# Second attention of a small vision tower: the maximum of slot 1 is subtracted by TensorE in PSUM instead of by VectorE, and VectorE copies that slot's transposes

## What is computed

```python
def _L1_attn_ref(x, edge_index, edge_attr, Wq, bq, Wk, bk, Wv, bv, Wo, bo, We, be):
    q = (x @ Wq + bq).reshape(B, N, H, hd)          # B=8 images, N=64 tokens, H=8 heads, hd=8
    k = (x @ Wk + bk).reshape(B, N, H, hd)
    v = (x @ Wv + bv).reshape(B, N, H, hd)
    scores = jnp.einsum('bihd,bjhd->bhij', q, k) / jnp.sqrt(jnp.asarray(hd, x.dtype))
    scores = scores + col_bias[None, :, None, :]     # from edge_attr @ We + be
    attn = jax.nn.softmax(scores, axis=-1)
    out = jnp.einsum('bhij,bjhd->bihd', attn, v).reshape(B, N, D)
    return out @ Wo + bo

h = _L0_tok_ref(...)                       # patch embedding and positions
h = h + _L0_attn_ref(_layernorm(h), ...)   # first attention
h = h + _L0_ffn_ref(_layernorm(h), ...)    # routed feed-forward
h = h + _L1_attn_ref(_layernorm(h), ...)   # second attention: here
h = h + _L1_ffn_ref(_layernorm(h), ...)    # top-2 mixture of 8 experts
```

## Time and profile before

| | |
|---|---|
| median of 3 runs | 74.75 us (74.56 to 74.87) |
| the profiled execution | 74.51 us |
| its span, first to last instruction | 72.7 us |
| outside the span | 1.8 us |
| PE busy | 64.6 us, 89% of the span |
| DVE busy | 41.9 us, 58% |
| ACT busy | 29.2 us, 40% |
| POOL busy | 13.0 us, 18% |
| granted TensorE clock, mean | 0.992 |

### The profile page before, as it was taken

One profiled execution on the slowest core, in us unless ns is written; L12 is line 12 of the kernel. 1 busy time (PEld: TensorE's weight loads), 2 busy tenths in 40 slices (PEclk: granted clock), 3 DMA queues, 4 the chain that ended last, 5 costly groups with the idle time before them and its releaser, 6 DMA issues.

```text
span 72.7 us, 1994 instructions
## 1 busy us (share of the span) xinstructions
PE 64.6 (89%) x843; PEld 39.5 (54%) x843; DVE 41.9 (58%) x108; ACT 29.2 (40%) x63; POOL 13.0 (18%) x29
## 2 busy tenths in 40 slices
PE   3995996999999999989979969799999889999930
PEld 1330554777887585445435645577954285543910
DVE  2590199484799983536642397997540157429430
ACT  0330104404497821296925060488023748530030
POOL 6800094000004920538030000000000030000000
PEclk9999999999999999999999999999999999999996
DMA  0799999900000000000000000000000000000003
GB/s 5 180 394 390 373 224 263 265 16 0 0 9 0 0 9 0 0 0 5 0 0 0 0 0 9 0 9 0 0 9 5 0 0 0 0 0 0 0 0 72
DMA packets 2389, 4.07 MB, mean 56 GB/s; under 512 B 779, under 2 KB 1229, under 8 KB 2381
## 3 DMA queue, kind: packets, MB, share of 16 engines
q1 hardware_dynamic: 1840, 3.55, 16.8%
q10 hardware_dynamic: 509, 0.40, 1.7%
q0 software_dynamic: 32, 0.00, 0.1%
HBM read 3.82 MB, written 0.13 MB: 54 GB/s over the span
## 4 chain that ended last, share of the span: by engine, by line
PE 64%; DVE 13%; DMA 9%; ACT 4%; POOL 3%; issue 3%; DVEq 0%; ACTq 0%; POOLq 0%
PE psum L687 10%; DMA Xt<-in_x_dram 9%; PE psum L681 6%; DVE top L503 3%; POOL WoS L298 3%; PE psum L697 3%; PE psum L893 3%; PE psum L939 3%; PE psum L789 3%; PE psum L740 3%; PE psum L991 3%; PE psum L1032 2%; PE psum L716 2%; DVE E L601 2%; DVE top L599 2%
## 5 line engine op out<-in xcount | busy, mean ns | idle before, releaser
L687 PE MATMUL psum<-warm 128*128 128x512 bf16 x63 | 19.9, 429 | 1.2 <-DVE warm L455 1.2
L687 PEld LDWEIGHTS psum<-warm 128*128 128x128 bf16 x63 | 5.8, 107 | 8.1 <-issue 4.3
L298 POOL TENSOR_TENSOR WoS<-pack_attn,top 128x256 f32<-128x256 f32 x5 | 3.1, 647 | 11.1 <-DVE top L510 11.1
L468 DVE TENSOR_TENSOR onehot<-idb,iota 128x2048 bf16<-128x2048 bf16 x4 | 4.8, 1244 | 0.0
L326 POOL TENSOR_TENSOR resT<-hT,xC 128x256 f32<-128x256 f32 x1 | 0.7, 724 | 20.5 <-DVE xC L630 20.5
L405 ACT ACTIVATE E<-E 128x512 f32<-128x512 f32 x4 | 2.5, 630 | 3.2 <-DVE E L601 3.1
L348 ACT ACTIVATE lv<-psum,eps 128x256 f32<-128x256 f32 x4 | 1.9, 473 | 3.5 <-PE psum L729 0.9
L599 DVE TENSOR_REDUCE top<-psum 128x8 f32<-128x512 f32 x4 | 2.7, 686 | 0.4 <-PE psum L908 0.4
L434 ACT ACTIVATE ge<-psum,pack_moe 128x512 f32<-128x512 f32 x4 | 2.5, 679 | 1.1 <-PE psum L991 1.1
L908 PE MATMUL psum<-kT,qT 9*64 9x64 f32 x128 | 2.1, 231 | 0.9 <-DVE qT L587 0.7
L773 PE MATMUL psum<-top,pack_ident 128*128 128x256 f32 x12 | 2.9, 387 | 0.0
(11 more groups left out here) (200 smaller groups left out, 131.7 us busy)
## 6 DMA issues: line engine op xcount, KB each, us to landing
Xt<-in_x_dram SPq DMA_DIRECT2D x1, 1024.0 KB, 6.4
Xt<-in_x_dram SPq DMA_DIRECT2D x1, 512.0 KB, 7.5
pack_both<-in_both_dram SPq DMA_DIRECT2D x2, 240.2 KB, 8.8
pack_moe<-in_moe_dram SPq DMA_DIRECT2D x1, 450.0 KB, 9.8
pack_mid<-in_mid_dram SPq DMA_DIRECT2D x1, 327.5 KB, 10.0
pack_attn<-in_attn_dram SPq DMA_DIRECT2D x1, 288.0 KB, 8.1
pack_expert<-in_expert_dram SPq DMA_DIRECT2D x2, 130.0 KB, 9.3
pack_wp<-in_wp_dram ACTq DMA_DIRECT2D x1, 192.0 KB, 6.0
```

The source lines that it names most:

```text
L298: gp.tensor_tensor(WoS[:, s, 4 * u:4 * u + 4, :].rearrange("p (b n) d -> p b n d", b=2), bc(WoT[:, 2 * u:2 * u + 2, :], 1, 2), bc(top0[:, ...
L468: ve.tensor_tensor(onehot[:, 16 * k:16 * k + 16, :], bc(idb[:, k, :], 1, 16), iota16[:, :, :], ALU.is_equal).then_inc(s_hot, 1)
L687: mm(B[bank][:, :], lhsT=warm[:, 0:P], rhs=warm[:, :], start=True, stop=True)
```

## The change

Slot 1 alone is treated differently. DVE takes its maximum with the sign turned (`negate`), and does not subtract. A new function `shift1()` on PE, behind `scores1(1)`, multiplies the identity with the negated maximum into banks 0 to 3, columns 128 to 255, accumulating onto the scores. The scores products therefore set their start flag only for the first block of a bank. ACT's `exp1(1)` waits for `shift1()` and reads PSUM. Because PSUM then holds slot 1's scores until that exponential is done, the transposes of slot 0 (bank 2) and `values1` (banks 0 and 1) wait for `exp1(1)`. ACT does `exp1(2)` before `et_copy(0)`; `et_copy(1)` leaves ACT and becomes a DVE copy behind the last subtraction. Two `keep_clock` calls, three dummy products together, are gone.

```diff
@@ ACT @@
             def exp1(s):
-                act.wait_ge(s_sub1, s + 1)
-                sc.activation(E1[:, s, :, :], E1[:, s, :, :], ACT.Exp).then_inc(s_exp1, 1)
+                if s == 1:
+                    act.wait_ge(s_sub1p, 1)
+                    sc.activation(E1[:, 1, :, :].rearrange("p (q g) t -> p q g t", g=2),
+                                  psum[:, 0:4, P:2 * P].rearrange("p q (g t) -> p q g t", t=TOK), ACT.Exp).then_inc(s_exp1, 1)
+                else:
+                    act.wait_ge(s_sub1, max(s, 1))
+                    sc.activation(E1[:, s, :, :], E1[:, s, :, :], ACT.Exp).then_inc(s_exp1, 1)
...
             exp1(0)
             exp1(1)
+            exp1(2)
             et_copy(0)
-            exp1(2)
-            et_copy(1)
             exp1(3)
             et_copy(2)
@@ DVE @@
-                ve.tensor_reduce(top, S, X, ALU.max).then_inc(s_mx1, 1)
+                ve.tensor_reduce(top, S, X, ALU.max, negate=(s == 1)).then_inc(s_mx1, 1)
+                if s == 1:
+                    return
                 dve.wait_ge(s_mx1, s + 1)
                 ve.tensor_tensor(E1[:, s, :, :].rearrange("p (q g) t -> p q g t", g=2), S, bc(top, 3, TOK),
                                  ALU.subtract).then_inc(s_sub1, 1)
...
+            dve.wait_ge(s_et, 2)
+            ve.tensor_copy(ET[:, 1, :, :].rearrange("p q n -> p (q n)"), B[3][:, :]).then_inc(s_et_ev_v, 1)
             dve.wait_ge(s_v1, 2)
@@ PE @@
-                                         rhs=kT1[rows_, g, tok:tok + TOK], start=True, stop=True)
+                                         rhs=kT1[rows_, g, tok:tok + TOK], start=(j == 0 and g == 0), stop=(c == 1),
+                                         skip_group_check=True)
...
+            def shift1():
+
+                pe.wait_ge(s_mx1, 2)
+                for hh in range(4):
+                    ins = mm(B[hh][:, P:2 * P], lhsT=ident, rhs=bc(top1[:, 1, 2 * hh:2 * hh + 2], 2, TOK), start=False, stop=True,
+                             skip_group_check=True)
+                ins.then_inc(s_sub1p, 1)
...
             def values1(c):
-                pe.wait_ge(s_sub1, 2)
+                pe.wait_ge(s_exp1, 2)
...
             def context(c):
...
-                    if s < 3:
-                        pe.wait_ge(s_et_ev_a, s + 1)
+                    if j == 0:
+                        pe.wait_ge(s_et_ev_a, c + 1)
                     else:
-                        pe.wait_ge(s_et_ev_v, 1)
+                        pe.wait_ge(s_et_ev_v, c + 1)
...
             scores1(1)
-            pe.wait_ge(s_sub1, 2)
+            shift1()
+            pe.wait_ge(s_exp1, 2)
             probsT(0)
-            keep_clock(3, 2)
             probsT(1)
             values1(0)
             values1(1)
             pe.wait_ge(s_et_ev_a, 1)
-            keep_clock(2, 1)
             probsT(2)
-            pe.wait_ge(s_sub1, 4)
+            pe.wait_ge(s_sub1, 3)
             pe.wait_ge(s_h2, 1)
             mm(B[6][:, 0:HALF], lhsT=centre[:, :], rhs=hT[2][:, :], start=True, stop=False, skip_group_check=True)
-            pe.wait_ge(s_et_ev_a, 2)
+            pe.wait_ge(s_et_ev_v, 1)
             probsT(3)
```

More of the change, by code:

```diff
@@ L222, in vit_tower @@
         s_v1, s_v1_ev = sem("v1_ps"), sem("v1_ready")
-        s_sc1, s_mx1, s_sub1, s_exp1 = sem("scores1_ps"), sem("max1_done"), sem("shifted1"), sem("exp1_done")
+        s_sc1, s_mx1, s_sub1, s_sub1p, s_exp1 = (sem("scores1_ps"), sem("max1_done"), sem("shifted1"), sem("shifted1_ps"),
+                                                 sem("exp1_done"))
         s_q1_v = sem("q1_ready_dve")
@@ L403, in exp1 @@
             def exp1(s):
-                act.wait_ge(s_sub1, s + 1)
-                sc.activation(E1[:, s, :, :], E1[:, s, :, :], ACT.Exp).then_inc(s_exp1, 1)
+                if s == 1:
[5 more added lines that the diff above has]
+                    sc.activation(E1[:, s, :, :], E1[:, s, :, :], ACT.Exp).then_inc(s_exp1, 1)
             def et_copy(s):
                 act.wait_ge(s_et, s + 1)
-                bank = B[2 + s % 2]
-                sc.activation(ET[:, s, :, :].rearrange("p q n -> p (q n)"), bank[:, :], ACT.Copy).then_inc(s_et_ev_a, 1)
+                sc.activation(ET[:, s, :, :].rearrange("p q n -> p (q n)"), B[2][:, :], ACT.Copy).then_inc(s_et_ev_a, 1)
             exp1(0)
             exp1(1)
+            exp1(2)
             et_copy(0)
-            exp1(2)
-            et_copy(1)
             exp1(3)
```

## The result

The changed kernel takes 77.83 us in the median of four runs (77.47 to 78.84), the kernel before 74.66 beside it (74.56 to 74.87). The ratio is 1.040 (95% interval 1.036 to 1.045), so the change costs 3.0 us, between 2.7 and 3.4. I had said 75.7, at most 76.3: the direction was right, the size wrong by a factor of three.

The account below looks back on a forecast made before the run. It took PE's own work and DVE's softmax, meeting at 50.6, to bound the context stage. Transposes 1.62 later, less 0.66 for dummies, gave +0.96 on 74.75: 75.7, range 75.2 to 76.3.

Parts of the forecast that it names:

- The change's path: On PE ahead of slot 0's transposes: products 1.07, exponential 0.60, wake-up 0.06; 1.62 later, less 0.66 for dummies, +0.96.
- The factor of four: Identity products on PE: by the skill each costs four transposes, 1.76 in all; fell in the dearer-products rival, 8 in 100.
- VectorE gains nothing: DVE's softmax: the removed subtraction's 0.69 becomes idle time, since the third maximum waits for scores1(1); gain taken as 0.
- TensorE's dummies are worth nothing before: Context stage before the change: PE's own work and DVE's softmax, nearly equal in length, meet at 50.6.
- The new waits behind it: Behind slot 0's transposes: DVE's copies and bias additions and ACT's work have 0.5 us or more to spare, adding nothing.
- Clock: Rival: TensorE's clock falls in PE's hole from 48.0 to 48.7; up to 79, or 77 if partly; 5 in 100.
- what the sum puts behind the context: nothing: Behind context(0): nothing hides or adds to the delay, and everything is shifted by the same +0.96.
- rival of a shorter pause: Pause inside scores1(1) gone: DVE's chain 0.5 shorter, 74.25 only if PE's chain also shrinks, otherwise +0.5; 4 in 100.

Follow-up runs that it names:

- e12: Changed kernel with only two of the four identity products and one single-element ScalarE activation more: 75.31 us, ratio 1.008 to the kernel before.
- e14: Changed kernel with twelve tiny TensorE dummies more ahead of the router logits and one single-element ScalarE activation more: ratio 1.012 to the kernel before.
- e4: Kernel before the change, without the three dummies between the transposes: 75.04 us, ratio 1.002.
- e3: Changed kernel with slot 1's subtraction given back to VectorE, all else of the change kept: 75.42 us, ratio 1.006 to the kernel before.
- e8: Kernel before the change, without the six dummies ahead of scores1(1): 76.20 us, ratio 1.017.
- e7: Changed kernel with one dummy fewer ahead of scores1(1) and one single-element ScalarE activation more: profiled execution 76.87 us at a clock of 0.977.
- e9: Changed kernel with one single-element ScalarE activation more behind et_copy(2): profiled execution 77.90 us at a clock of 0.975, another 75.56 at full clock.
- e13: Changed kernel with twelve tiny dummies more ahead of the router logits, where TensorE waits: profiled execution 76.88 us at a clock of 0.977.
- e15: Kernel before the change, with twelve tiny dummies more ahead of the router logits, where TensorE waits: profiled execution 74.99 us.
- e2: Changed kernel without five dummies around the second layer norm, where TensorE waits anyway: profiled execution 76.24 us.
- e6: Changed kernel with one dummy fewer ahead of scores1(1): 77.45 us, ratio 1.034 to the kernel before.

## Why the prediction was right and wrong

**The change's path: right, to 0.03.** Identity products, exponential, wake-up, less three dummies: +0.96 forecast, +0.99 in the trace, and half of the products give 0.45 back (`e12`). That it came as near as 0.03 is in part luck, since small errors cancelled. The products took 1.16 instead of 1.07 (I had built on the 0.63 of four transposes in the earlier trace rows; the four there that stood behind a wait took 0.66), but they started 0.05 earlier behind the scores, and the exponential with its hand-overs took 0.69 instead of 0.70. From the transposes on it was 3.39 (49.33 to 52.72), as forecast. With the side effects out the ratio gives 0.9, within 0.5 to 1.2 (`e14`), which agrees but would not tell 0.96 from 0.6. The factor of four that the Trainium skill gives for the transpose mode ("TensorE: Matmul & The Clock Gate", its section "Terms") would have made the products 1.76 and does not hold: four of them took 1.16, as eight records do, and eight transposes took 1.09.

**VectorE gains nothing, TensorE's dummies are worth nothing before: right.** The third maximum still waits for the scores, and `e4` measured 1.002.

**The new waits behind it: right.** Neither the bias additions nor VectorE's copies hold `context` up. In `e3`, with the subtraction on VectorE, the later copy of slot 0 shows as a wait of 0.64, inside slack.

**Clock: not the cause.** It is 1.00 through the stage, in a hole of 0.69. A hole of 1.95 does bring it down (`e8`).

**The step that failed is what the sum puts behind the context: nothing.** The prediction says that "the chain goes on from it through PE, DVE and ACT in turn" and that everything behind `context(0)` is "shifted by the same amount". The runs showed 0.31 more there at the logarithm and 1.4 to 1.5 more at the end, so 1.7 to 1.8 in place of 0, and this alone takes 75.7 out of the range. The step counted work and waits and left out the instructions themselves. The change moves TensorE's list by eleven instructions and ScalarE's by one, and two costs hang on places in these lists:

- ScalarE stands for about 0.31 at a fixed place of its list. Before, that place lay in a wait. One instruction fewer moved it into the wait for the variance product, beyond its end. An instruction more takes it back (`e7`, `e9`, `e12`, `e14`). That this standing is the request for the next instruction packet is my reading of the packet that moves with it; no run separates the two.
- A seventh 16 KB packet of instructions, of 1.3 to 1.5, meets the results on their way and makes their wait 2.5 to 2.7 instead of 1.3. Sent 1.8 to 2.5 us ahead of them it costs nothing (`e13`, `e14`, `e15`), and with ten instructions less it was not there (`e2`, one trace). Over all traces the late end came with a packet at 72.7 to 73.1 (the changed kernel, `e6`, `e9`) and in no other.

Together 0.99 + 0.31 + 1.4 = 2.7 of the 3.0 that the ratio gives, which its interval just takes in. `e6`, with the same three parts, has 2.6 by its ratio. What remains of the 3.0 is noise or the pause in the scores; in the two traces, 3.4 apart, the pause makes 0.53. It was 0.27 in the trace of before, the shortest of all with a pause; in the other traces it was 0.30 to 0.84 (1.95 in `e8`), and in four there was none. I had called it a thing that nothing explains, and took the trace's 0.27 as given. It ends 1.26 after a 16 KB instruction packet has landed in both traces (45.35 and 46.61 before, 45.93 and 47.19 after), and 1.2 to 1.5 after it in all thirteen traces with a pause. In the four without one that packet had landed 2.4 us or more before the second scores began. I read this as TensorE having run out of instructions. The packet's moment differs between executions, so I take the pause's length as chance, common to both kernels; that was not tested by itself. The prediction's rival of a shorter pause had its size right: with scores 0.45 earlier it gave the change +0.5, and the one trace of a changed kernel at full clock without a pause shows 0.42 (`e14`). So a part of the change's cost depends on when that packet comes.

**Open.** What decides whether the seventh packet is sent near 72.8 or not at all before the end, when the list has 1740 to 1743 instructions. Length, ScalarE's count and dummies behind the end were each ruled out as the one cause. It came in all four executions of `e6` by their times, and, as far as times and traces tell, in some and not in others of `e7` and `e9`. Why the place of ScalarE's instruction costs 0.31, and what sets the moment of TensorE's fourth packet, is open too.

## What to carry to other kernels

Moving work from a full engine to another gains only if the next item of the full engine is ready: here VectorE's next maximum waited for the scores, and the saved 0.69 became idle time, while the moved work sat in series on TensorE. Add up not only an edit's work but its instructions on every list: a pause that hangs on a place in the list can slide out of a wait into the path, and an instruction packet at the end of the program can meet the results. When a change costs more than its own path, compare the distance from the last computation to the end and the queue of instruction packets first; a few dummies or a one-element activation in a wait tell quickly whether places in the list are to blame.

## What was not expected of the hardware

- While a single 16 KB instruction packet was under way, two sends of 64 KB each landed 1.2 to 1.4 us later (the changed kernel, `e6`, `e9`). Their small packets were then spread over 1.9 to 2.1 us instead of 0.9. That both use the same DMA engines is the likely reason; the packet records don't name the engine.
- TensorE, fed with many small products, stops in the middle of a run of them, for 0.27 to 0.84 us here (1.95 in `e8`), always at the same place of its list, and goes on 1.2 to 1.5 us after an instruction packet has landed.
- One hole of 1.95 us on TensorE halved its clock for the next 6 us (`e8`), where holes of 0.69 and 0.77 had done nothing.
